# Last batch of a two-layer graph kernel: second-layer rows 512 to 1023 in two column parts, last store in two transfers

## What is computed

```python
# layer 0: mean over neighbours, concatenated with x, one product, relu
deg = sum(adj, -1);  agg = adj @ x / max(deg, EPS)
x = layernorm(x + relu(concat([x, agg]) @ W.T))
# layer 1: degree-normalised adjacency with self loops
Ah = adj + eye;  dh = rsqrt(sum(Ah, -1))
x = layernorm(x + relu(((dh * Ah * dh.T) @ x) @ kernel + bias))
```

## Time and profile before

| | us |
|---|---|
| median of three executions (lowest, highest) | 509.39 (509.22, 509.75) |
| profiled execution, its own time | 509.72 |
| its span, first to last instruction | 507.5 |
| PE busy | 494.9 (98% of the span) |
| DVE busy | 388.8 (77%) |
| ACT busy | 243.9 (48%) |
| share of PE in the chain that ended last | 95% |

### The profile page before, as it was taken

One profiled execution on the slowest core, in us unless ns is written; L12 is line 12 of the kernel. 1 busy time (PEld: TensorE's weight loads), 2 busy tenths in 40 slices (PEclk: granted clock), 3 DMA queues, 4 the chain that ended last, 5 costly groups with the idle time before them and its releaser, 6 DMA issues.

```text
span 507.5 us, 8749 instructions
## 1 busy us (share of the span) xinstructions
PE 494.9 (98%) x3086; PEld 446.8 (88%) x3086; DVE 388.8 (77%) x1021; ACT 243.9 (48%) x483; POOL 0.7 (0%) x6
## 2 busy tenths in 40 slices
PE   8999999999999999999999999999999999999992
PEld 6998889988899888998899988998889988899872
DVE  4897489885798667985879849798498974798556
ACT  6836427364364544455363543636427364263312
POOL 0000000000000000000000000000000000000000
PEclk9999999999999999999999999999999999999998
DMA  8943402714036230563107440154401614020002
GB/s 295 404 175 111 167 0 87 261 67 165 0 135 237 75 131 0 171 226 112 69 0 240 173 164 2 41 210 162 165 0 41 248 41 166 0 84 1 1 0 83
DMA packets 18666, 59.78 MB, mean 118 GB/s; under 512 B 1760, under 2 KB 1888, under 8 KB 18656
## 3 DMA queue, kind: packets, MB, share of 16 engines
q1 hardware_dynamic: 18656, 59.64, 33.1%
HBM read 51.25 MB, written 8.39 MB: 118 GB/s over the span
## 4 chain that ended last, share of the span: by engine, by line
PE 95%; DVE 2%; DMA 1%; ACT 1%; SPq 0%; issue 0%; ACTq 0%
PE ring_a L629 24%; PE ring_a L633 12%; PE ring_b L645 11%; PE ring_b L646 11%; PE ring_b L647 11%; PE ring_b L588 5%; PE ring_b L587 5%; PE ring_b L586 5%; PE ring_a L586 3%; PE ring_a L587 3%; PE ring_a L588 3%; DMA xt_raw<-xT 1%; DVE u L424 0%; DVE stats L433 0%; DVE x L428 0%; DVE xt_lo L364 0%
## 5 line engine op out<-in xcount | busy, mean ns | idle before, releaser
L629 PE MATMUL ring_a<-z_hi,adj_lo 128*128 128x258 f32 x512 | 103.2, 283 | 0.0
L629 PE MATMUL ring_a<-z_hi,adj_hi 128*128 128x258 f32 x512 | 102.5, 282 | 0.0
L633 PE MATMUL ring_a<-z_lo,adj_hi 128*128 128x256 f32 x512 | 101.3, 279 | 0.0
L645 PE MATMUL ring_b<-adj_hi,x1s_hi 128*128 128x512 f32 x256 | 99.9, 390 | 0.0
L646 PE MATMUL ring_b<-adj_lo,x1s_hi 128*128 128x512 f32 x256 | 99.7, 389 | 0.0
L647 PE MATMUL ring_b<-adj_hi,x1s_lo 128*128 128x512 f32 x256 | 99.7, 389 | 0.0
L629 PEld LDWEIGHTS ring_a<-z_hi,adj_lo 128*128 128x128 f32 x512 | 79.2, 189 | 0.0
L633 PEld LDWEIGHTS ring_a<-z_lo,adj_hi 128*128 128x128 f32 x512 | 79.0, 189 | 0.0
L629 PEld LDWEIGHTS ring_a<-z_hi,adj_hi 128*128 128x128 f32 x512 | 78.0, 188 | 0.1
L364 DVE TENSOR_TENSOR adj_lo<-adj_raw,adj_hi 128x1024 fp32r<-128x1024 f32 x64 | 75.0, 1221 | 3.6 <-ACT adj_hi L238 2.7
L238 ACT ACTIVATE adj_hi<-adj_raw 128x1024 fp32r<-128x1024 f32 x64 | 62.8, 1056 | 0.0
(11 more groups left out here) (75 smaller groups left out, 693.6 us busy)
## 6 DMA issues: line engine op xcount, KB each, us to landing
adj_raw<-adjT SPq DMA_DIRECT2D x64, 512.0 KB, 6.0
x_sb<-x SPq DMA_DIRECT2D x16, 512.0 KB, 5.1
out<-x SPq DMA_DIRECT2D x16, 512.0 KB, 2.7
xt_raw<-xT SPq DMA_DIRECT2D x7, 1024.0 KB, 5.4
x<-w SPq DMA_DIRECT2D x2, 256.0 KB, 3.4
xt_raw<-xT SPq DMA_DIRECT2D x2, 256.0 KB, 3.8
xt_raw<-xT SPq DMA_DIRECT2D x1, 512.0 KB, 6.1
x<-k SPq DMA_DIRECT2D x1, 256.0 KB, 9.4
```

What stands on the lines that cost most here:

```text
L629: nc.tensor.matmul(ring_a[:, t % NB + o, 0:F + 2], adj_block(a, h, j, i0 + o * P, P), z_hi[:, j, :], start=(j == 0 and a is a_hi), stop=False)
L633: last = nc.tensor.matmul(ring_a[:, t % NB + o, 0:F], adj_block(a_hi, h, j, i0 + o * P, P), z_lo[:, j, :], start=False, stop=(j == T - 1))
L645: nc.tensor.matmul(ring_b[:, bank, :], lhi, ahi, start=(j == 0), stop=False)
```

## The change

In the last batch alone, half 1 of the second layer's propagation is computed in two column parts of 256 (rows 512 to 767 of the graph, then 768 to 1023). Part 0 goes to banks 0 and 1 of `ring_b` as before, part 1 to banks 2 and 3 of `ring_a`. Source tiles 0 to 3 come first, as before, now in four groups of 12 matmuls (part 0, then part 1 behind a wait on `agg_read`) in place of two. With source tiles 4 to 7, behind the same 24 matmuls for half 0, PE's order is: part 0, feature half 0; `project1` of tiles 0 to 3; part 0, feature half 1; part 1, both feature halves; then `project1` of tiles 4 and 5, and of 6 and 7, each two behind their own wait on `g_read`. Tiles with t % 4 of 2 or 3 are projected into `ring_b` in place of `ring_a`. ACT and DVE have four reads of 256 columns for half 1 in place of two of 512, placed by hand in DVE's new `finish`. The last four tiles go out in two transfers of two tiles, the two that DVE normalises first. Batches 0 to 6 issue the same instructions in the same order as before (`add_pair` and `stats_pair` are `add_layer1` cut in two; what is left out of the diff only takes the `if more` away from their code).

```diff
@@ -16,6 +16,7 @@
...
+PART = (slice(0, NH // 2), slice(NH // 2, NH))
...
@@ -169,6 +170,14 @@
             return (g1_hi if hi else g1_lo)[:, f, :]
+        def last_g1(f, c):
+            return ring_b[:, f, 0:NH // 2] if c == 0 else ring_a[:, 2 + f, 0:NH // 2]
+        def last_ring(t):
+            return ring_a if t % NB < 2 else ring_b
...
@@ -217,10 +226,12 @@
                 batch(b, True)
             batch(B - 2, False)
             store(B - 1, 0)
-            sp.wait_ge(last_out_done, 1)
-            store(B - 1, 1)
+            for first, ready, n in ((T - 2, last_out_done, 1), (TH, out_done, B * H)):
+                sp.wait_ge(ready, n)
+                sp.dma_start(out[B - 1, :, first:first + 2, :],
+                             x1[:, first:first + 2, :]).then_inc(x1_free[1], 16)
             for h in range(H):
-                sp.wait_ge(x1_free[h], 16 * (B + 1))
+                sp.wait_ge(x1_free[h], 16 * (B + 1 + h))
...
@@ -298,6 +309,10 @@
                 act.wait_ge(g_done, b * 4 + n + 1)
                 copy(g_part(True, h, f), ring_b[:, bank, :]).then_inc(g_hi_done, 1)
+            def read_last_g1(b, n, f, c):
+                act.wait_ge(g_done, b * 4 + n + 1)
+                copy(g_part(True, 1, f)[:, PART[c]], last_g1(f, c)).then_inc(g_hi_done, 1)
...
@@ -319,22 +334,26 @@
                 diagonal(b, 1)
                 read_g(b, 0, 0, 0, 2)
                 read_g(b, 1, 0, 1, 3)
-                if more:
-                    split_adj(b + 1, 0, b * 4 + 2)
+                if not more:
+                    read_last_g1(b, 2, 0, 0)
+                    read_last_g1(b, 3, 1, 0)
+                    read_last_g1(b, 4, 0, 1)
+                    root(b, 2, TH)
+                    read_last_g1(b, 5, 1, 1)
+                    norm1(b, 0)
+                    root(b, 3, TH)
+                    norm1(b, 1, range(TH // 2))
+                    return
...
                 read_g(b, 2, 1, 0, 0)
-                if more:
-                    root(b, 2, TH)
+                root(b, 2, TH)
                 read_g(b, 3, 1, 1, 1)
-                if not more:
...
@@ -415,23 +434,32 @@
...
+            def add_pair(b, h, q, ring=lambda t: ring_a):
+                t = h * TH + q
+                for o in range(2):
+                    dve.wait_ge(proj1_done, b * T + t + o + 1)
+                    nc.vector.scalar_tensor_tensor(
+                        u1[:, o, :], ring(t + o)[:, (t + o) % NB, 0:F], dh[:, h, q + o:q + o + 1],
+                        bias_sb[:], ALU.mult, ALU.add).then_inc(proj1_read, 1)
+                dve.wait_ge(proj1_read, b * T + t + 2 + T)
+                nc.vector.scalar_tensor_tensor(
+                    x1[:, t:t + 2, :], u1[:, :, :], 0.0, x1[:, t:t + 2, :],
+                    ALU.max, ALU.add).then_inc(resid1_done, 1)
...
+            def stats_pair(b, h, q):
+                t = h * TH + q
+                dve.wait_ge(resid1_done, b * (T // 2) + t // 2 + 1)
+                for o in range(2):
+                    last = nc.vector.bn_stats(stats[:, q + o, :], x1[:, t + o, :])
+                if q == TH - 2:
+                    last.then_inc(stats_done, 1)
...
@@ -483,6 +511,11 @@
                 dve.wait_ge(g_hi_done, b * 4 + n + 1)
                 minus(g_part(False, h, f), ring_b[:, bank, :], g_part(True, h, f)).then_inc(g_read, 1)
+            def read_last_g1(b, n, f, c):
+                dve.wait_ge(g_hi_done, b * 4 + n + 1)
+                minus(g_part(False, 1, f)[:, PART[c]], last_g1(f, c),
+                      g_part(True, 1, f)[:, PART[c]]).then_inc(g_read, 1)
...
@@ -511,34 +544,48 @@
                 diagonal(b, 1)
                 read_g(b, 0, 0, 0, 2)
                 read_g(b, 1, 0, 1, 3)
-                if more:
-                    split_adj(b + 1, 0)
-                    add_identity(0)
+                if not more:
+                    finish(b)
+                    return
...
-                if not more:
-                    read_g(b, 3, 1, 1, 1)
                 variances(b, 2, 0)
...
+            def finish(b):
+                read_last_g1(b, 2, 0, 0)
+                add_pair(b, 0, 0, last_ring)
+                stats_pair(b, 0, 0)
+                add_pair(b, 0, 2, last_ring)
+                read_last_g1(b, 3, 1, 0)
+                stats_pair(b, 0, 2)
+                variances(b, 2, 0)
+                read_last_g1(b, 4, 0, 1)
+                inverse_roots(b, 2, TH, rstd1[:], rstd1[:])
+                read_last_g1(b, 5, 1, 1)
+                for q in range(0, TH, 2):
+                    add_pair(b, 1, q, last_ring)
+                    stats_pair(b, 1, q)
+                variances(b, 3, 0)
+                inverse_roots(b, 3, TH, rstd1[:], rstd1[:])
+                dve.wait_ge(nb_done, b * 4 + 4)
+                for q in range(TH // 2, TH):
+                    last = nc.vector.tensor_scalar(x1[:, TH + q, :], x1[:, TH + q, :],
+                                                   rstd1[:, q:q + 1], nb[:, q:q + 1],
+                                                   ALU.mult, ALU.add)
+                last.then_inc(last_out_done, 1)
...
@@ -636,22 +683,23 @@
                         if j == T - 1:
                             last.then_inc(agg_done, 1)
-            def propagate(h, f, bank, sources):
+            def propagate(h, f, o, sources, rows=slice(0, NH)):
                 cols = slice(f * P, (f + 1) * P)
+                i0, n = rows.start, rows.stop - rows.start
                 for j in sources:
                     lhi, llo = x1s_hi[:, j, cols], x1s_lo[:, j, cols]
-                    ahi, alo = adj_block(a_hi, h, j, 0, NH), adj_block(a_lo, h, j, 0, NH)
-                    nc.tensor.matmul(ring_b[:, bank, :], lhi, ahi, start=(j == 0), stop=False)
-                    nc.tensor.matmul(ring_b[:, bank, :], lhi, alo, start=False, stop=False)
-                    last = nc.tensor.matmul(ring_b[:, bank, :], llo, ahi, start=False, stop=(j == T - 1))
+                    ahi, alo = adj_block(a_hi, h, j, i0, n), adj_block(a_lo, h, j, i0, n)
+                    nc.tensor.matmul(o, lhi, ahi, start=(j == 0), stop=False)
+                    nc.tensor.matmul(o, lhi, alo, start=False, stop=False)
+                    last = nc.tensor.matmul(o, llo, ahi, start=False, stop=(j == T - 1))
                 if sources[-1] == T - 1:
                     last.then_inc(g_done, 1)
-            def project1(t):
+            def project1(t, ring=ring_a):
                 h, cols = t // TH, slice((t % TH) * P, (t % TH + 1) * P)
-                product(ring_a[:, t % NB, 0:F],
+                product(ring[:, t % NB, 0:F],
                         [(g_part(True, h, f)[:, cols], g_part(False, h, f)[:, cols],
                           k_hi[:, f, :], k_lo[:, f, :]) for f in range(FT)]).then_inc(proj1_done, 1)
...
@@ -683,33 +731,52 @@
                         for j in range(first, first + TH):
                             if f == 0:
                                 pe.wait_ge(x1s_lo_done, b * T + j + 1)
-                            propagate(0, f, 2 + f, [j])
+                            propagate(0, f, ring_b[:, 2 + f, :], [j])
                     if first == 0 and not more:
-                        for f in range(FT):
-                            pe.wait_ge(g_read, b * 4 + 3 + f)
-                            propagate(1, f, f, range(TH))
-                if more:
-                    pe.wait_ge(z_lo_done, b * T + T + 5)
+                        for c in range(2):
+                            for f in range(FT):
+                                if c == 0:
+                                    pe.wait_ge(g_read, b * 4 + 3 + f)
+                                else:
+                                    pe.wait_ge(agg_read, b * T + T)
+                                propagate(1, f, last_g1(f, c), range(TH), PART[c])
+                if not more:
+                    finish(b)
+                    return
+                pe.wait_ge(z_lo_done, b * T + T + 5)
                 pe.wait_ge(diag_lo_done, b * H + 2)
-                rest = range(0 if more else TH, T)
-                propagate(1, 0, 0, rest)
+                propagate(1, 0, ring_b[:, 0, :], range(T))
                 pe.wait_ge(k_lo_done, 1)
                 pe.wait_ge(g_read, b * 4 + 2 + 4)
                 for t in range(TH):
                     pe.wait_ge(agg_read, b * T + TH + t + 1)
                     project1(t)
-                if more:
-                    pe.wait_ge(z_lo_done, b * T + T + 6)
-                propagate(1, 1, 1, rest)
-                if more:
-                    for t in range(PL, T):
-                        pe.wait_ge(g_read, b * 4 + t - PL + 1 + 4)
-                        project0(b + 1, t, t % NB)
+                pe.wait_ge(z_lo_done, b * T + T + 6)
+                propagate(1, 1, ring_b[:, 1, :], range(T))
+                for t in range(PL, T):
+                    pe.wait_ge(g_read, b * 4 + t - PL + 1 + 4)
+                    project0(b + 1, t, t % NB)
```

(59 more changed lines are left out.)

1 line of the change is left out of this document (removed).

## The result

The changed kernel takes 508.04 us (median of 10, 507.77 to 509.06) against 509.48 in the same comparison: ratio 0.9977, 95% interval 0.9967 to 0.9986, or 1.2 us less (0.7 to 1.7). The ratio goes by the means of the two groups (508.2 and 509.4), so it gives less than the difference of the medians, 1.44. Its profiled execution took 507.77 us with a span of 506.0. Executions of one kernel differ by about 1 us. In the traces this difference arises ahead of PE's 101st matmul, which starts 20.8 to 22.0 us into the span; from there to P it is 447.3 us in every one.

A forecast was written before the change was run, and what follows sets the result against it. The prediction took DVE's list of work at the end to bound the kernel, PE close behind. 509.72 (profiled execution) - 1.30 (column parts) - 0.30 (stores) = 508.1, so a median of 507.8 us from 509.39, range 507.2 to 508.8.

The forecast's parts named there:

- Which chain bounds the end: End of the last batch: DVE's list of work from about 489 us sets the end, with PE close behind.
- The idle time of 1.41 goes, a wait of 0.15 comes: PE, last batch: 1.41 us idle before the last projections vanishes; a 0.15 us wait appears before projecting tile 0.
- Two narrow ones cost 0.2365: PE: two 256-column matmuls at 0.118 us spacing cost 0.0095 us more than one of 512 columns.
- DVE's list: DVE's last-batch schedule with four cut reads: the pair after tiles 4 and 5 starts 1.30 us earlier.
- give back more: Rival, chance 0.12: DVE reads overlap less or the square root comes late; 508.3 us, or 508.6 with the root late.
- the square root does not wait for ACT: Sign on DVE's normalisation: a root waiting for ACT, busy in a read, would show the forecast wrong; 0.3 us late.
- The stores. Gain 0.30: Last store in two transfers: data end 0.35 us earlier, shorter rows give back 0.05, gain 0.30 us.
- the first rival: Chance 0.14: the split store gains nothing or costs up to 0.2 us; 508.1 to 508.3 us.
- both need 1.30 at the rate of before: Last store: the two transfers' data together move in 1.30 us, as the single 512 KB transfer did.
- the landing 0.5 behind the data: Last store: before the change, the transfer landed 0.5 us after its data had moved.
- The transfers go one behind the other: Rival, chance 0.07 including combination with DVE's rival: second transfer served only after the first lands, +0.95 us, 509.0 us.
- Slower, paced by the weight loads: Rival, chance 0.03: 96 narrow matmuls spaced by 0.188 us weight loads, 514.5 us; decisive from a 0.135 spacing on.

The follow-up runs named there:

- e6: e2 plus one unused 256-column DVE read of PSUM ahead of part 1's last read; last batch's first propagation matmul to last normalisation 33.52 us (one execution).
- e7: e2 without eight high-by-low matmuls of part 1, source tiles 4 to 7; last batch's first propagation matmul to last normalisation 33.17 us (one execution).
- e8: Kernel before with only the 48 wide matmuls of half 1 in the last batch cut into 96 narrow ones; 510.40 us, ratio 1.0015.
- e1: Kernel before with only the last store cut into the changed kernel's two transfers; 509.98 us, ratio 1.0011.
- e5: Kernel before, last store in two transfers of two tiles, both issued after ACT and DVE finish; start of last normalisation to end 4.95 us (one execution).
- e4: Kernel before, last store in two transfers of 64 partitions, all four tiles in each; start of last normalisation to end 5.37 us (one execution).
- e10: Kernel before, only ACT's two reads of half 1 in the last batch cut in two; first propagation matmul to last normalisation 34.48 us (one execution).
- e2: Changed kernel with the last four tiles stored in one transfer again; 507.93 us, ratio 0.9968 to before.
- e3: e2 with DVE's last half reordered so that fewer dependent instructions directly follow their source; 507.88 us, ratio 0.9968 to before.
- e9: Kernel before with only half 1's reads in the last batch cut into 256 columns, on ACT and DVE; 509.14 us, ratio 0.9993.
- e11: Kernel before, only DVE's two reads of half 1 in the last batch cut in two; first propagation matmul to last normalisation 34.47 us (one execution).
- e12: e3 with ACT normalising only columns 0 to 127 of tile 5 and DVE the rest; 507.63 us, ratio 0.9963 to before.

## Why the prediction was right, and where it was not

The forecast of 507.8 with a range of 507.2 to 508.8 held (508.04). Its sum was -1.30 - 0.30 = -1.6; the runs have -1.09 for the parts, +0.28 for the stores and -0.37 beyond the span, -1.2 together, as by the ratio. So the mechanism of the column parts was right, but that the number was met so closely is luck: a gain of 0.37 that the prediction has no term for stands in for a gain of the stores that did not come. Without it the kernel would gain 0.8 us, less than the 1.02 that the prediction counts as a difference.

- *Which chain bounds the end*: right. e6 and e7 bracket it: DVE and PE meet within 0.15 us at tile 5, and behind it DVE's list bounds.
- *The idle time of 1.41 goes, a wait of 0.15 comes*: right, by the rows.
- *"Two narrow ones cost 0.2365"*: mis-sized. The spacing was taken from the projections (0.118); the narrow propagations come every 0.120, in the changed kernel and in e8. PE came to tile 4 at P + 25.52, where the forecast has 25.32. Of these 0.20, 0.09 arise over the 48 narrow matmuls of the first sources (5.75 in place of 5.66) and 0.07 over the 36 ahead of tile 4 (4.32 in place of 4.25); 0.04 is left for the changes between wide and narrow and the reads. The 12 others lie under the new wait. All of the 0.20 reaches tile 5, where PE and DVE meet; this is the 0.2 missing from the 1.30.
- *DVE's list*: right. u of tile 4 came 1.22 earlier (forecast 1.33; PE had tile 0 ready 0.12 later than forecast), the read under the square root cost 0.02, the one ahead of the statistics 0.2, as forecast. So DVE does not give back more, and the square root does not wait for ACT.
- *"The stores. Gain 0.30"*: this step failed, and the first rival, no gain or a small cost, is what happened (0.28, a little over its 0.2). The early start came as worked out. What failed is "both need 1.30 at the rate of before" (1.6 measured) and the landing 0.5 behind the data (0.9 measured). DMA: Bandwidth & Descriptors in the Trainium skill (section Anatomy of one DMA, on the other kind of queue) gives each transfer a large fixed cost beside that of its bytes. The trace agrees in that: 256 KB land 2.5 and 2.9 us behind their issues and 512 KB 2.6, so halving the bytes brings little or nothing. The same page of the Trainium skill (section Bandwidth) advises to batch transfers, and e1 and e5 bear it out, with 0.28 and 0.70 us lost. Why the second of two lands later behind its data, no run here tells.
- *The transfers go one behind the other*: did not happen. The data have no hole, and the second lands at N + 4.07, where this rival has D + 3.99, which is N + 4.73.
- *Slower, paced by the weight loads*: did not happen; 0.120 is far below its 0.135.
- *What lies around the span is the same*: assumed without a word, and false by 0.37 us. This more than made up for the store's loss.

## What to carry to other kernels

A last store in two transfers pays only if the head start of the first is worth more than the second transfer costs; here the cost was 0.70 us, and a head start of 0.42 gave 0.43 of it back. What was left was the second transfer's longer landing, which an earlier first transfer does not touch. Where two engines meet at the end of a program, a price off by 0.002 us per instruction counts as soon as a hundred of them stand ahead of the meeting, so take it from rows with the same operands. On DVE what depends on the instruction ahead of it started about 0.1 us later here than what does not (0.72 and 0.61 behind x), and independent work put between the two took that out.

## What the hardware showed that I had not expected

The time beyond the span, which is what the whole execution takes more than the profile's first to last instruction, is steady within 0.07 us for a kernel (of which 0.05 is the rounding of the spans), but changes by up to 0.38 us with DVE's program: it is 2.16 to 2.21 with 1021 DVE instructions executed (before, e1, e4, e5, e8, e10), 1.80 to 1.81 with 1023 (changed, e2, e3, e7, e9, e11), and 1.93 to 1.94 with 1024 (e6, e12). 48 more matmuls (e8), a second transfer (e1) or two more ACT instructions (e10) do not move it. Whether the count itself matters or something that goes with it, and whether the time lies ahead of the span or behind it, no run here tells. In a comparison of less than 1 us it is as large as the effects looked for.
